# Token lists of an expert layer built with 16-bit floats and one wide comparison, in a four-layer kernel

## What is computed

```python
gate_logits = xf @ w_gate                       # 2048 x 4
topk_logits, topk_idx = jax.lax.top_k(gate_logits, 2)
gates = jax.nn.softmax(topk_logits, axis=-1)
hmid = gelu(einsum('tc,ech->eth', xf, w1) + b1)  # 4 experts, 288 -> 1152
eo = einsum('eth,ehc->etc', hmid, w2) + b2       # 1152 -> 288
moe = einsum('te,etc->tc', cw, eo)
x = x + g_mlp * moe
```

## Time and profile before

| | us |
|---|---|
| median of 3 runs | 1563.07 (1561.31 to 1564.18) |
| profiled execution | 1574.09 |
| its span, first to last instruction | 1572.4 |
| mean granted TensorE clock in it | 0.966 of full |

### The profile page before, as it was taken

One profiled execution on the slowest core, in us unless ns is written; L12 is line 12 of the kernel. 1 busy time (PEld: TensorE's weight loads), 2 busy tenths in 40 slices (PEclk: granted clock), 3 DMA queues, 4 the chain that ended last, 5 costly groups with the idle time before them and its releaser, 6 DMA issues.

```text
span 1572.4 us, 26968 instructions
## 1 busy us (share of the span) xinstructions
PE 1450.9 (92%) x9013; PEld 991.7 (63%) x9013; DVE 1229.0 (78%) x2563; ACT 930.4 (59%) x1687; POOL 715.3 (45%) x1621
## 2 busy tenths in 40 slices
PE   7899999978999999893999999899899999989998
PEld 5653334866999888782743334788785333468885
DVE  7789996887798587655889997677887999876643
ACT  4458886534566454573468888344644888754432
POOL 0565640115455533126666666676766666640000
PEclk9999999998999999996999999999998999999999
DMA  8765530116655544436545531201065454100001
GB/s 213 225 164 126 145 75 2 42 35 204 185 152 134 154 116 129 123 94 195 176 128 136 133 75 6 47 5 21 5 173 184 117 143 107 7 2 1 1 1 61
DMA packets 107606, 158.87 MB, mean 101 GB/s; under 512 B 33860, under 2 KB 75830, under 8 KB 107336
## 3 DMA queue, kind: packets, MB, share of 16 engines
q1 hardware_dynamic: 101964, 142.32, 30.2%
q0 software_dynamic: 5504, 14.83, 8.1%
HBM read 113.43 MB, written 39.06 MB: 97 GB/s over the span
## 4 chain that ended last, share of the span: by engine, by line
PE 59%; DVE 16%; issue 3%; ACT 2%; another core or an unknown queue 1%; POOL 0%; DMA 0%; DVEq 0%; ACTq 0%; POOLq 0%
PE psum L1631 20%; PE psum L1821 8%; PE psum L2107 7%; PE psum L1810 6%; PE psum L1784 6%; PE psum L2248 5%; PE psum L1694 1%; DVE bn L2458 1%; DVE x_norm L2486 1%; DVE hid_lo L3158 1%; PE psum L1960 1%; PE psum L2388 1%; PE psum L2080 1%; PE psum L2285 1%
## 5 line engine op out<-in xcount | busy, mean ns | idle before, releaser
L1550 ACT ACTIVATE probs<-psum 128x512 f32<-128x512 f32 x768 | 401.8, 600 | 85.5 <-PE psum L1810 85.0
L2646 DVE TENSOR_REDUCE minus_max<-psum 128x1 fp32r<-128x512 f32 x450 | 288.7, 683 | 32.9 <-PE psum L1784 31.5
L1631 PE MATMUL psum<-x_split,w_hi 128*128 128x512 f32 (+1 forms) x684 | 246.7, 404 | 13.5 <-issue 6.6
L1784 PE MATMUL psum<-k_stack,q_stack 54*128 54x512 f32 x768 | 245.6, 454 | 9.2 <-DVE minus_max L2646 2.7
L1810 PE MATMUL psum<-q_stack,k_stack 55*128 55x512 f32 x768 | 243.0, 449 | 0.6 <-ACT probs L1550 0.6
L1081 POOL TENSOR_TENSOR qr_m<-qr_m 64x8 f32<-64x8 f32 (+35 forms) x544 | 195.7, 360 | 42.6
L1821 PE MATMUL psum<-probs,o_t 128*19 128x512 f32 x1536 | 205.8, 608 | 6.1 <-ACT o_t L1529 3.2
L2641 DVE TENSOR_REDUCE minus_max<-psum 128x2 fp32r<-128x1024 f32 x159 | 193.9, 1220 | 19.4 <-PE psum L1784 19.2
L1784 PEld LDWEIGHTS psum<-k_stack,q_stack 54*128 54x128 f32 x768 | 116.1, 188 | 130.2 <-DVE minus_max L2646 62.1
L1810 PEld LDWEIGHTS psum<-q_stack,k_stack 55*128 55x128 f32 x768 | 118.5, 187 | 126.3 <-ACT probs L1550 115.3
L1076 POOL TENSOR_TENSOR qr_m<-qr_rows 64x288 f32<-64x288 f32 (+31 forms) x64 | 45.5, 711 | 243.5 <-DMA qr_rows<-qr_rows 243.5
(11 more groups left out here) (433 smaller groups left out, 3274.3 us busy)
## 6 DMA issues: line engine op xcount, KB each, us to landing
qk_parts_d<-qk_parts SPq DMA_DIRECT2D x48, 512.0 KB
raw_b<-in_L_cond_w SPq DMA_DIRECT2D x36, 432.0 KB, 4.6
q_stack<-qk_parts_d SPq DMA_DIRECT2D x96, 144.0 KB
k_stack<-qk_parts_d SPq DMA_DIRECT2D x96, 144.0 KB
raw_a<-in_L_cond_w SPq DMA_DIRECT2D x36, 384.0 KB
q_stack<-qk_parts_d SPq DMA_DIRECT2D x96, 72.0 KB
k_stack<-qk_parts_d SPq DMA_DIRECT2D x96, 72.0 KB
moe_out_d<-branch SPq DMA_DIRECT2D x9, 576.0 KB, 3.6
```

The costliest lines, as they stand in the source:

```text
L1550: act.activation(PE_[:, v // 4, 2 * hf + pr, :], psum[:, score_bank(16 * i + v), :], ACT.Exp, scale=SCALE).then_inc(s_e, 1)
L1631: i = pe.matmul(dst, a, r, start=(n == 0), stop=(n == len(terms) - 1))
L1784: return pe.matmul(psum[:, bank, :], Q6[half(hf, STK), g, pr, P * qt:P * qt + P], K6[half(hf, STK), g, pr, :], start=True, stop=True)
L2646: dve.tensor_reduce(MX[:, i % 2, col:col + 1], psum[:, bank, :], AX.X, ALU.max, negate=True).then_inc(s_mx, 1)
```

## The change

- Hit masks are 16-bit floats with ten bits of fraction (`F16`) in place of bf16; token numbers up to 2047 are exact in them. So the lists need one product of 64 columns and no sum of two halves. The row mask carries the token number (`TKN`, one scalar per partition and tile), and the eight column masks of a batch are made by one comparison over 8 x 64 elements. The split of all slots is done once, in `split_slots`.
- `tokens(b)` gathers all batches in one sum in PSUM, begun by a product with zeros (`RTS[:, 0]`), so `first_tokens` is one cast.
- `rows_x` writes the tail three times into `moe_x`; `moe_rows_d` has 352 columns, the gathers fetch all, and `first_tails` and `tile_tails` are gone. `turn_first` waits for each quarter's transfer, and ahead of quarter 2 for `s_ff`, now set in `tile_places` once the expert counts are read from PSUM.
- The order: `list_hits(0)` to `(3)` come behind units 0 to 3, the list products into iterations 2 to 4, `token_lists` to unit 3; `tile_table` comes ahead of unit 0; `logits` waits chunk by chunk; `ranks(3)` comes ahead of `tokens(2)`; fewer dummy products.
- SyncE loads tile 1's b2 and the first third of its w1 and w2 as soon as the tile table is made, ahead of the token lists.

The diff, without its smaller hunks (widths of slices, semaphore counts), shifted left:

```diff
@@ -167,16 +167,16 @@
-TKV = at("token_parts", [P, NT, 2], BF16, rb + 53312)
-HOT = [at(f"slot_hits{i}", [P, TT, N], BF16, ra + 9728 * i) for i in range(2)]
-ROWHIT = [at(f"list_rows{i}", [P, TT, 2, P], BF16, xo + 4096 * i) for i in range(2)]
-COLHIT = [at(f"list_columns{i}", [P, TT, 2, 2, LISTS], BF16, xo + 4096 * i + 2048) for i in range(2)]
+TKV = at("token_numbers", [P, NT, 2], F16, rb + 53312)
+HOT = [at(f"slot_hits{i}", [P, TT, N], F16, ra + 9728 * i) for i in range(2)]
+ROWHIT = [at(f"list_rows{i}", [P, TT, 2, P], F16, xo + 4096 * i) for i in range(2)]
+COLHIT = [at(f"list_columns{i}", [P, TT * 2, LISTS], F16, xo + 4096 * i + 2048) for i in range(2)]
...
-TKN = at("token_in_tile", [P, 1], F32, xo + 28160)
+TKN = at("token_scale", [P, NT], F32, xo + 28160)
...
-XMR = [at(f"moe_x{b}", [P, TT, C], F32, xo + o) for b, o in enumerate((0, 8192, 16384, 22016))]
+XMR = [at(f"moe_x{b}", [P, TT, XNW], F32, xo + o) for b, o in enumerate((0, 8192, 16384, 22016))]
@@ -273,9 +273,9 @@
-SPLIT = new("slot_split", [P, 2, TT, 2], I32)
-SPLITF = new("slot_places", [P, B, 2, TT, 2], F32)
-LISTF = new("token_lists_f", [P, LISTS], F32)
+SPLIT = new("slot_split", [P, 2, NT, 2], I32)
+SLOTROW = new("slot_rows", [P, NT, 2], F32)
+SLOTCOL = new("slot_columns", [P, NT, 2], F16)
@@ -814,11 +813,13 @@
+        load_tile_b2(1, e)
+        load_tile_w1(1, 0, e)
+        load_tile_w2(1, 0, e)
...
-        load_tile_b2(1, e)
-        for i in range(3):
+        for i in (1, 2):
@@ -1149,7 +1149,7 @@
-        gp.iota(TKN[:, :], pattern=[[0, 1]], base=0, channel_multiplier=1, allow_small_or_imprecise_dtypes=True).then_inc(s_cn, 1)
+        gp.iota(TKN[:, :], pattern=[[P, NT]], base=0, channel_multiplier=1, allow_small_or_imprecise_dtypes=True).then_inc(s_cn, 1)
...
     def gather_rows(t):
@@ -1164,7 +1164,7 @@
         for q in range(quarters(t)):
-            gp.indirect_dma_start(out=XROW[t % 2][:, q, 0:C], out_offset=None, in_=XTD[:, :],
+            gp.indirect_dma_start(out=XROW[t % 2][:, q, :], out_offset=None, in_=XTD[:, :],
...
     def gather(k, b):
@@ -1299,7 +1299,12 @@
-            act.activation(XMR[b][:, :, P * c:P * c + n], psum[:, FRONT_BACK[c], 0:TT * n].rearrange("p (t n) -> p t n", t=TT), ACT.Copy).then_inc(s_xc, 1)
+            src = psum[:, FRONT_BACK[c], 0:TT * n].rearrange("p (t n) -> p t n", t=TT)
+            if c < KC:
+                act.activation(XMR[b][:, :, P * c:P * c + n], src, ACT.Copy).then_inc(s_xc, 1)
+            else:
+                act.activation(XMR[b][:, :, KC * P:XNW].rearrange("p t (r n) -> p t r n", r=3),
+                               src.unsqueeze(2).to_broadcast([P, TT, 3, TAIL]), ACT.Copy).then_inc(s_xc, 1)
...
     def first_hi(h, c):
@@ -1995,7 +2000,6 @@
     def logits(b):
...
-        pe.wait_ge(s_xf, 3 * b + 3)
@@ -2006,6 +2010,7 @@
+            pe.wait_ge(s_xf, 3 * b + c + 1)
@@ -2044,29 +2049,33 @@
-                mm = pe.matmul(psum[:, 3, 0:2 * LISTS], ROWHIT[b % 2][:, t, k, :], COLHIT[b % 2][:, t, k, :, :].rearrange("p a c -> p (a c)"),
+                mm = pe.matmul(psum[:, 3, 0:LISTS], ROWHIT[b % 2][:, t, k, :], COLHIT[b % 2][:, 2 * t + k, :],
...
     def turn_first():
...
         for q in range(TT):
-            pe.wait_ge(s_ff, q + 1)
+            if q == 2:
+                pe.wait_ge(s_ff, 1)
+            pe.wait_ge(s_fr[q], 16)
...
-                keep_clock(0, 2)
+                keep_clock(0, 1)
...
     def tokens(b):
...
+        if b == 0:
+            pe.matmul(psum[:, 1, 0:TT], IDN[:, :], RTS[:, 0, :], start=True, stop=False)
...
         for q in range(TT):
-            c = 8 * b + 2 * q
...
-                mm = pe.matmul(psum[:, 1, c:c + 2], HOT[b % 2][:, t, P * q:P * q + P], TKV[:, TT * b + t, :], start=(t == 0), stop=(t == TT - 1))
+                mm = pe.matmul(psum[:, 1, q:q + 1], HOT[b % 2][:, t, P * q:P * q + P], TKV[:, TT * b + t, 0:1],
+                               start=False, stop=(b == B - 1 and t == TT - 1 and q == TT - 1))
...
     def turn_tile(t, c):
@@ -2074,7 +2083,7 @@
-            pe.wait_ge(m_xt, t)
+            pe.wait_ge(m_x[t % 2], rows_landed(t))
...
         for q in range(quarters(t)):
@@ -2097,8 +2106,6 @@
-        if j == 0:
-            pe.wait_ge(s_tb, 1)
         for q in range(quarters(t)):
@@ -2166,22 +2173,20 @@
         turn_back(2)
         turn_logits(2)
         ranks(1)
-        keep_clock(3, 2)
         turn_x(3)
-        keep_clock(3, 4)
+        keep_clock(3, 3)
         logits(3)
-        turn_back(3)
         ranks(2)
         turn_logits(3)
+        turn_back(3)
         tokens(0)
         tokens(1)
-        list_products(0)
-        keep_clock(0, 4)
+        keep_clock(0, 1)
+        ranks(3)
         tokens(2)
-        ranks(3)
-        keep_clock(0, 5)
+        keep_clock(0, 3)
         tokens(3)
-        keep_clock(0, 12)
+        keep_clock(0, 9)
         turn_first()
         for j in range(MOE_UNITS + 2):
             t, m = divmod(j, HM)
@@ -2191,10 +2196,9 @@
-            if j == 0:
-                list_products(1)
-                list_products(2)
-            if j == 1:
+            if 2 <= j <= 4:
+                list_products(j - 2)
+            if j == 4:
@@ -2795,34 +2799,37 @@
     def first_tokens():
...
-        link(dve.tensor_reduce(TKF[:, :], psum[:, 1, 0:2 * TT * B].rearrange("p (b q k) -> p q b k", q=TT, k=2), AX.XY, ALU.add))
-        dve.tensor_copy(TIX[0][:, :], TKF[:, :]).then_inc(s_t0, 1)
-    def list_hits(b):
-        rows, cols = ROWHIT[b % 2], COLHIT[b % 2]
-        dve.wait_ge(s_ix, b + 1)
-        slots_ = IDX[:, TT * b:TT * b + TT, :].bitcast(I32)
+        dve.tensor_copy(TIX[0][:, :], psum[:, 1, 0:TT]).then_inc(s_t0, 1)
+    def split_slots():
+        slots_ = IDX[:, :, :].bitcast(I32)
+        dve.wait_ge(s_ix, B)
...
-        link(dve.tensor_copy(SPLITF[:, b, :, :, :], SPLIT[:, :, :, :]))
+        dve.tensor_copy(SLOTROW[:, :, :], SPLIT[:, 0, :, :])
+        link(dve.tensor_copy(SLOTCOL[:, :, :], SPLIT[:, 1, :, :]))
+    def list_hits(b):
+        rows, cols = ROWHIT[b % 2], COLHIT[b % 2]
+        shape = [P, TT * 2, LISTS]
...
-            dve.wait_ge(s_cn, 9)
+            dve.wait_ge(s_cn, 8)
...
+            i = TT * b + t
...
-                row, col = SPLITF[:, b, 0, t, k:k + 1], SPLITF[:, b, 1, t, k:k + 1]
-                dve.tensor_scalar(rows[:, t, k, :], PLACE[:, :], row, None, ALU.is_equal)
-                dve.tensor_scalar(cols[:, t, k, 0, :], PLACE[:, 0:LISTS], col, float(P * (TT * b + t)), ALU.is_equal, ALU.mult)
-                i = dve.tensor_scalar(cols[:, t, k, 1, :], PLACE[:, 0:LISTS], col, TKN[:, 0:1], ALU.is_equal, ALU.mult)
-        i.then_inc(s_oh, 1)
+                dve.tensor_scalar(rows[:, t, k, :], PLACE[:, :], SLOTROW[:, i, k:k + 1], TKN[:, i:i + 1], ALU.is_equal, ALU.mult)
+        where = SLOTCOL[:, TT * b:TT * b + TT, :].rearrange("p t k -> p (t k)")
+        dve.tensor_tensor(cols[:, :, :], PLACE[:, 0:LISTS].unsqueeze(1).to_broadcast(shape),
+                          where.unsqueeze(2).to_broadcast(shape), ALU.is_equal).then_inc(s_oh, 1)
...
     def token_lists():
...
-        link(dve.tensor_reduce(LISTF[:, :], psum[:, 3, 0:2 * LISTS].rearrange("p (a c) -> p c a", a=2), AX.X, ALU.add))
-        dve.tensor_copy(LIST[:, :], LISTF[:, :]).then_inc(s_tl, 1)
+        dve.tensor_copy(LIST[:, :], psum[:, 3, 0:LISTS]).then_inc(s_tl, 1)
...
     def rows_stats(b):
@@ -2885,7 +2892,7 @@
-        dve.memset(M16[:, 0, 0:1], 1.0)
+        dve.memset(M16[:, 0, 0:1], 1.0).then_inc(s_ff, 1)
@@ -2971,13 +2973,6 @@
-    def tile_tails(t):
-        dve.wait_ge(m_x[t % 2], rows_landed(t))
-        q = slice(0, quarters(t))
-        for r in range(2):
-            i = dve.tensor_copy(XROW[t % 2][:, q, C + TAIL * r:C + TAIL * (r + 1)], XROW[t % 2][:, q, KC * P:C])
-        i.then_inc(m_xt, 1)
...
     def tile_low(t, c):
@@ -3066,44 +3061,37 @@
         logit_rows(2)
         slots(1)
         gate_ranks(2)
+        logit_rows(3)
         slot_hits(1)
-        list_hits(0)
-        logit_rows(3)
         slots(2)
         gate_ranks(3)
         slot_hits(2)
         slots(3)
         slot_hits(3)
+        split_slots()
         first_tokens()
         split_lo_first(0, "1", 0)
         split_lo_first(0, "2", 0)
         split_lo_first(0, "1", 1)
         tile_places()
-        for q in range(TT):
-            first_tails(q)
-        list_hits(1)
         for h in range(2):
             for c in range(KC + 1):
                 first_low(h, c)
-        list_hits(2)
-        list_hits(3)
+        tile_table()
         for j in range(MOE_UNITS):
             t, m = divmod(j, HM)
             tile_parts(j)
             if t >= 1 and m == 1:
                 tile_take(t - 1)
-            if t + 1 < TILES and m == turn_at(t) - 1:
-                tile_tails(t + 1)
             if t + 1 < TILES and 0 <= m - turn_at(t) <= KC:
                 tile_low(t + 1, m - turn_at(t))
-            if j == 0:
-                tile_table()
-            if j == 1:
```

(8 more changed lines are left out.)

24 lines of the change are left out of this document (9 added, 15 removed).

## The result

The changed kernel takes 1554.24 us (median of 20 runs, 1548.03 to 1559.62) beside 1561.42 for the kernel before (20 runs, 1556.58 to 1566.54): ratio 0.9956, 95% interval 0.9944 to 0.9968. That is 7.2 us faster; 12.5 were forecast, to 1550.6.

The account below looks back on a forecast made before the run. VectorE's queue, with gather waits, was taken to bound routing to unit 9 (tile 1's first hidden product). Unit 9 12.2 us earlier plus 0.3 makes 12.5: profiled 1574.09 becomes 1561.6, carried to the median 1550.6; range 1545.5 to 1558.0.

Parts of the forecast that it names:

- First leg, copy at 325.05: Routing to first token copy: list_hits(0) moved away 4.6, ranks(3) earlier 1.9, less 0.1; 6.4 us won.
- Second leg, unit 0 at 336.05: Token copy to unit 0: gather 8.55 us plus 2.45 behind its last landing, 11.0 us; unit 0 11.2 us earlier.
- Third leg, the lists at 354.9: VectorE from unit 0 to the token lists: 19.0 us, list_hits 2.5 each; lists ready at 354.9, not 361.43.
- Third leg, the rows at 365.3: Tile 1's gather: 2.7 us from lists to first issue, 7.7 to last landing; transpose 10.1 us earlier.
- Fourth leg, 11.2 us to unit 9: Tile 1's first transpose to unit 9: 11.2 us instead of 13.3; unit 9 at 376.5, 12.2 us earlier.
- rival A: New waits before tile 1's transpose halve the clock (2.5 us more), list_hits cost 3.4; gain 6.4 to 10, 1555 us; chance 0.24.
- the tail copies' 0.3: Tail copies removed in VectorE-bound tiles 8 to 10: 0.3 us won beyond unit 9's 12.2.
- B: Clock holds ahead of unit 9, 2.5 us more, and fast wide comparison, 1.4 more: 1547 us; chance 0.10.
- C: Clock stays at 1.2 GHz through all of tile 0, nine slow units: 3.6 us slower, 1566.7; chance 0.04.
- D: Something behind unit 9 (output stores, GpSimd reflectors or rotation) takes the gain back: 1563 us; chance 0.04.

Follow-up runs that it names:

- c_after: The changed kernel itself, run again as the measure for its neighbours on the same chip: 1568.87 us beside 1577.42 for the kernel before, ratio 0.9948.
- e_clock_kept: The changed kernel plus 20 identity products on TensorE ahead of tile 1's first transpose: 1551.97 us, ratio 0.9941 to the kernel before.
- e_lists_alone: The kernel before with only the change's cheap token lists, order, stored rows and loads as before: 1554.40 us, ratio 0.9961 to the kernel before.
- e_rows_first: The changed kernel with the last two thirds of tile 1's weights issued only after its rows land: 1564.38 us, ratio 0.9928 to the kernel before.
- e_lists_first: The changed kernel with the token lists ahead of the two weight splits in unit 3: 1561.27 us, ratio 0.9898 to the kernel before.
- e_lists_again: A repeat of the changed kernel with the token lists ahead of unit 3's two weight splits: 1550.31 us, ratio 0.9923 to the kernel before.
- e_lists_few: The changed kernel with token lists ahead of unit 3's two splits and 6 identity products before tile 1's first transpose: 1543.14 us, ratio 0.9875 to before.
- after: The changed kernel in its first measurement and profile, against the kernel before: 1554.24 us, ratio 0.9956.
- e_no_reflector: The changed kernel without its thirteenth Householder step on GpSimd (Q not the reference's): 1550.86 us, ratio 0.9947 to the kernel before.
- e_weights_late: The changed kernel with tile 1's b2 and first weight thirds again loaded behind the token lists: 1569.55 us, ratio 0.9967 to the kernel before.
- e_order_alone: The changed kernel with the list comparisons of the kernel before, all else as changed: 1562.73 us, ratio 0.9992 to the kernel before.
- e_lists_clock: The changed kernel with token lists ahead of unit 3's two splits and 20 identity products before tile 1's first transpose: 1545.73 us, ratio 0.9914 to before.
- e_lists_rows: The changed kernel with token lists ahead of unit 3's two splits and three of tile 1's weight loads behind its rows: 1546.68 us, ratio 0.9904 to before.

## Why the prediction was right in direction and too large

**First leg, copy at 325.05 (63.35 from the mark).** Right where the clock held. The copies of the kernels in the new order fall in two groups, at 63.1 to 63.3 (seven executions) and at 64.8 to 65.0 (five). The instructions are the same; in the late group TensorE's clock is lower already when ranks(3) runs. VectorE's row behind it, and the windows, in c_after and in e_clock_kept:

```profile
321.62 0.18 DVE L2868 TENSOR_TENSOR slots<-psum,ramp 128x16 f32<-128x16 f32 x1 [0.41 <-PE psum L2039]
...
318.00:322.00 4.00, 3.44 (x65) 3.04 (x65) 3.27 (x17) 4.00 (x7) 0.00 (x0) 1.00 0.48 180
```

```profile
323.18 0.18 DVE L2871 TENSOR_TENSOR slots<-psum,ramp 128x16 f32<-128x16 f32 x1 [1.64 <-PE psum L2039]
...
318.00:322.00 4.00, 3.45 (x48) 3.00 (x46) 3.23 (x17) 4.00 (x8) 0.00 (x0) 0.80 0.48 180
```

It waits 0.41 us or 1.64, and for tokens(3) 0.27 or 0.79: together 1.75 us. The forecast knew only the first. That the clock products taken out have to do with it isn't shown: e_lists_alone has all those of before, and its clock fell early as well. One bound was mispriced without harm: six clock products at 0.24 us each were put at 1.4 us, but a product is two passes, and five of them took 2.40 us at 327.83 in before, so six are 2.9.

**Second leg, unit 0 at 336.05.** It came at 335.84, 11.0 us behind the copy, as worked out, released by the x_tail subtraction.

**Third leg, the lists at 354.9.** They came at 353.92. The wide comparison takes 0.68 us (0.70 worked out) and eight row comparisons 1.87 (1.8). The Trainium skill (VectorE: DVE Perf Modes, "What auto-detection actually checks") asks for 16 bits and a step of one in every tensor before an operation on two tensors runs at two elements a cycle, and one operand here has step zero. The 684 ns for 512 elements agree: 480 elements in 32-bit floats took 659. Unit 5 waits 2.40 us (2.5 worked out). Up to here the steps hold within 1 us.

**Third leg, the rows at 365.3.** Here is the first failed step: "7.7 from first issue to last landing, as in the first gather". It was 10.8 to the transpose that waits for it, because the first gather ran with the DMA engines nearly idle (share 0.14) and this one beside the weight loads (0.83). The same two numbers come out of one pair of kernels that differ only in when those loads are issued: e_rows_first, 7.52, and c_after, 10.74. Some 3.1 us of the gain go here. The rows of before had a warning: tile 1's gather stood beside loads there too (0.74), and from its first issue to the transpose were 11.3 us, so nothing showed it landing in 7.7.

**Fourth leg, 11.2 us to unit 9.** The second failed step: 13.60 and 13.64. At the full clock, with GpSimd clear of VectorE, the leg is 10.84 to 10.87 in four executions (e_lists_first, e_lists_again, e_clock_kept, e_lists_few), better than worked out. So what was worked out holds, and two costs were left out, in different shares in the two executions.

The half clock behind the wait for the rows is one. From the transpose to the w_lo ahead of unit 9 are 8.39 us in e_clock_kept, 10.09 in after and 11.17 in c_after (rows above): 1.7 and 2.8 us. In c_after the half clock lasted longer; unit 7, from the transpose to unit 8's first product, took 4.06 us at the full clock, 5.75 in after and e_no_reflector, and 6.5 to 6.7 in c_after, e_weights_late and e_order_alone. The other is GpSimd: in after it drew out w_lo and hid_lo by 0.59 and 0.45 us, 1.0 together, and e_no_reflector, with the half clock but without that, is at 12.55. In c_after these two are not drawn out. That both executions come to 13.6 is chance. The leg of e_lists_clock (11.48) and e_lists_rows (11.77), at the full clock, holds 0.8 and 0.9 us of VectorE operations drawn out beside the same step.

TensorE stood 4.43 to 5.84 us ahead of that transpose in the executions that lost the clock and 2.80 or less in those that kept it; before, 4.59 us of idleness had cost it at unit 9. This is no threshold: in after the clock fell behind 2.40 us ahead of unit 5 as well (0.59 from 354 to 357), and behind 2.87 and 2.88 us ahead of unit 9 it held in two executions and fell in two (e_lists_first and e_lists_again, e_lists_few and e_clock_kept).

The half clock is rival A's mechanism (5.7 instead of 3.2 us for a unit, "2.5 more"), which I gave 0.24 although its trigger, 3.9 us of new idleness, was in my own sum. That the measured time, 1554.24, is rival A's 1555 is luck in part: A also needed `list_hits` at 3.4 us, and it took 2.5; the gather's 3.1 us, which no rival named, stand in its place.

**The sum.** Counted from the mark, the forecast starts the copy at 63.2, unit 0 at 74.4, the cast of the lists at 93.0, the transpose at 103.6 and unit 9 at 114.8. c_after is on it up to the lists (93.1), then 3.4 us late at the transpose and 5.8 at unit 9: 6.4 of 12.2 us are left. After had the late copy too (1.6 us), made up 0.6 on the lists and was 3.3 slower from there to the transpose and 2.4 in the last leg: 5.6 are left. At tile 2 the two are 6.3 and 6.1 us ahead of before. The medians say 7.2 and 8.5, so they hold 1 to 2.5 us more than these executions show, and the tail copies' 0.3 is the only part of it that was forecast. So 12.5 less 3.1 and 2.4 is 7.0, near the measured 7.2, but in part by luck: what the medians hold above the marks isn't explained.

**Rivals B, C, D.** B needed the clock and fast comparisons; the changed kernel has neither. C didn't come: tile 0's units ran at 1.00 from 340 to 354. D didn't come as a loss behind unit 9: from there to tile 2 are 12.2 us in before, 11.5 and 12.4 in after and c_after. But "hidden anyway" was true of two parts which the prediction counted into the same sum: the early weights (e_weights_late) and the order itself (e_order_alone, 0.9992). The prediction priced the order by unit 0, 11.2 us, and never asked what the rest would be worth without the cheap lists. Unit 9 hangs on tile table, lists, gather and places, all VectorE's work or behind it; moving the lists behind unit 0 shortens nothing of that. What shortens it is work removed: e_lists_alone, 0.9961, has the change's own 0.9956 within its interval.

**What stays open.** Why the clock falls before or behind 60 us from the mark in executions of the same instructions; what stops tile 6 for 4 to 6 us in some; and why the medians are often further under before than the marks of the profiled execution, most of all in e_lists_few, with 19.3 us beside 11.6 at unit 9 and 12.5 at tile 2. Its profile has no stop in tile 6, and yet that execution, 1549.64, is the slowest of its six. A smaller share of executions with the stop than before has would lower the median, but no run shows that share.

## What to carry to other kernels

When work is moved off one engine's path, follow the queue that the next late event hangs on to its end: an earlier start on TensorE is worth nothing if VectorE's total up to the next gather stays the same, and two edits that are priced together should also be priced alone. If the sum contains a new wait, give it the clock behind it as a cost, not as a rival; and a transfer takes the price that it had beside the same loads, not the one that it had alone. And put what starts a long transfer, here the token lists, ahead of any work that can run in its shadow: moving one call ahead of two gave another 4 to 8 us on top of the change's 7 to 8.5, by medians.

## What the runs showed of the hardware

- A gather of four 128-row quarters took 7.5 us from first issue to use with the DMA engines left to it (e_rows_first) and 10.1 to 11.1 in the eight executions that waited for it beside the same four weight loads.
- A product of the identity (128x128) in 32-bit floats is two passes in the trace: 20 products are 40 passes and 4.62 us, six are 12 and 1.50, both at a granted clock of 1.00, so 0.22 to 0.25 us a product.
- The granted clock fell behind 2.88 us of idleness ahead of unit 9 (e_lists_few, 0.66 in the 5 us from 377) and held behind 2.87 (e_lists_first, 1.00 in the 5 us from 378.6); a half clock there costs 1.5 us up to tile 2.
- VectorE's fp32r subtractions with both inputs in SBUF and GpSimd's 64x276 multiplications draw each other out. In after w_lo took 1.64 us and hid_lo 1.13 (rows above) beside the first of the two rows here; in c_after w_lo took 1.05 and hid_lo 0.68, and the second row, the same multiplication clear of VectorE's, 0.64:

```profile
378.65 1.45 POOL L1078 TENSOR_TENSOR qr_m<-qr_rows 64x276 f32<-64x276 f32 x1
```

```profile
375.28 0.64 POOL L1078 TENSOR_TENSOR qr_m<-qr_rows 64x276 f32<-64x276 f32 x1
```

The Trainium skill (SBUF — State Buffer, "SBUF: two separate sides") has VectorE instructions with two SBUF inputs and GpSimd's share one pair of ports by an exclusive lock, held for a whole instruction; these rows agree with it.
